# Two sixteen-head attentions of a four-layer kernel: which tick takes which PSUM bank, and when the reciprocals are transposed

## The chip, the cores and the metric

The kernel runs on one core of one Trainium2 chip. The metric is the device time of one launch in microseconds (us). TensorE, VectorE, ScalarE, GpSimd and the DMA queue of SyncE each run a program of their own and wait for each other through semaphores; in the rows of the profile they are PE (matmuls) and PEld (weight loads), DVE, ACT, POOL and SP.

## The reference, cut to what matters

Four layers of a network with adaptive layer norms. Each layer is an attention and then a feed-forward part, on 16 sequences of 256 tokens with 128 channels. The change concerns the attentions of layers 0 and 1, which have 16 heads of 64 channels each:

```python
h = _layernorm(x) * (1 + ca) + sa             # one (ca, sa) for each sequence
q, k, v = split(h @ wqkv.T)                    # 16 heads x 64, T = 256
# layer 0: q, k = rope(rmsnorm(q) * wq), rope(rmsnorm(k) * wk); causal mask
# layer 1: no norm of q and k; a relative-position bias is added to the scores
p = softmax(q @ k.T / 8 (+ bias))
x = x + ga * ((p @ v) @ wo.T)
```

## The kernel before, in words

`wide_attention(layer)` writes the program of one such attention; `causal` is true for layer 0. The 16 sequences are the outer loop, the 8 pairs of heads the inner one, and one pair of heads of one sequence is a **tick**: t = 0 to 127, and two more ticks to drain. u = t % 8 is the tick's place in its **octet**, k = t // 8 the octet, which is also the sequence whose scores are made. On every engine the body of the loop over t stands written out in program order, so the order of the work around the change is the order of the calls in that loop, and nothing else plans it.

In tick t TensorE does, in this order: `tensor_sums` (only at u = 1: it transposes the 128x32 tile RC of reciprocals of the softmax sums of the sequence before, one 128x128 operation into a bank of PSUM, line 570); `tensor_project` (q and k of a sequence that comes two octets later for layer 0, one octet later for layer 1: one matmul of 512 columns or two of 256); `tensor_turn` (layer 0 only: four 128x128 transposes of the rotated q or k, line 562); `tensor_extra` (see below); `scores` of pair t; `turn` of pair t - 1 (line 629: transposes of the exponentials, 12 in layer 0, 16 in layer 1); `value` of pair t - 2. The records of a 4-byte matmul come in twos, so that a 512-column matmul counts two.

`tensor_extra` holds what not every tick has: a quarter of the values v of the next sequence in the ticks u of `v_at` = (2, 3, 4, 7); the output projection of the sequence before, `c0` at u = 6 and `c1` at u = 7, eight matmuls each; and, in every second octet at u = 7, the turn of a normed chunk of x (two sequences, four 128x128 transposes, line 242), which is here called the norm's turn. `norm_at(a, u)` says when; a is the sequence that is being projected.

**The ring.** Banks 0 to 3 hold the scores, bank 4 the values' product. Everything else, so each project, turn, v, c0, c1, reciprocals' turn and norm's turn, goes into banks 5, 6 and 7 in rotation. `take_tick` hands them out, in its own order, when the program is written: the n-th taking gets bank 5 + n % 3, and a writer waits until the use of the same bank three takings before has been emptied. A tick of layer 0 takes two banks for project and turn and one for each extra, so u = 7 takes four (project, turn, v, c1) and in every second octet five; a tick of layer 1 takes one less.

VectorE's tick is `vector_spread` (u = 1: copies the transposed reciprocals out of PSUM, line 738, after which SyncE sends them to DRAM and back, spread over the partitions, lines 1037 and 1043), `vector_project` (layer 0: two multiplications of 128x512, line 713), `vector_extra` (the gated output at u = 6 and 7, line 168; the even quarters of v, line 772; for a chunk of the norm the statistics at u = 0, lines 176 and 179, and the normed x at u = 3 and 4, line 231), then the row maxima (lines 784, 785 and 787 in layer 0; 802 and 807 in layer 1), at u = 0 the reciprocals (line 748), the copy of half of the turned exponentials (line 869), and in layer 0 the sums of squares (line 729). ScalarE's tick is `scalar_turn`, `scalar_project` (layer 0: the squares; this frees the projection's bank), `scalar_extra` (the odd quarters of v; the modulation of the norm's turn), the other half of the turned exponentials, all on line 157, and then the four exponentials of the pair (line 932). GpSimd adds the rotated halves (lines 976, 977), scales k (line 997), raises the mean squares to the power -1/2 (line 985), scales the output with the reciprocals at u = 3 and 4 (line 1011, four of 128x512) and adds the residual (line 171).

Three waits matter for what follows:

```python
# scores(p): pair p - 2 must have left the banks      e.wait_ge(even_out, ...); e.wait_ge(odd_out, ...)
# turn(p):   the exponentials of pair p are made       e.wait_ge(pair_exped, p0 + p + 1)
# tensor_sums: the reciprocals are made                e.wait_ge(recip_made, b0 + c + 1)
```

Of the kernel before, what the change touches and what calls it, by code (L numbers as in the profile page):

```python
# [81 lines left out]
def program(nc, dr, out, stages=STAGES):  # L82
    ctx = ExitStack()
    with ctx:
# [323 lines left out]
        def wide_attention(layer, opening=None):  # L408
# [12 lines left out]
            causal = layer == 0  # L421
# [31 lines left out]
            ring = BK[5:8]  # L453
# [5 lines left out]
            ahead = 2 if causal else 1  # L459
            v_at = (2, 3, 4, 7)  # L460

# [8 lines left out]

            def norm_at(a, u):

                return u == 7 and a % 2 == 1 and a < 15

# [6 lines left out]
            def take_tick(t, a, b, u, ring=ring):  # L481

                for step, c in posts(t):
                    if step == "turn":
                        take(step, c, ring=ring)
                if 0 <= a < 16:
                    take("project", a, u, ring=ring)
                if causal and 0 <= b < 16:
                    take("turn", b, u, ring=ring)
                if 0 <= b < 16 and u in v_at:  # L490
                    take("v", b, v_at.index(u), ring=ring)
                for step, c in posts(t):
                    if step in ("c0", "c1"):
                        take(step, c, ring=ring)
                if norm_at(a, u):
                    take("ln", (a + 1) // 2, ring=ring)

# [74 lines left out]
            def tensor_extra(e, t, a, b, u):  # L572
                if 0 <= b < 16 and u in v_at:
                    tensor_v(e, b, v_at.index(u))
                for step, c in posts(t):
                    if step in ("c0", "c1"):
                        qt = int(step[1])
                        s = slots[step, c]
                        e.wait_ge(chunk_scaled, c0 + 4 * c + 4)
                        bk = fill(e, s)  # L580
                        for j in range(8):
                            x = mm(e, bk[:, 0:128], OT[(4 * c + j // 2) % 6][:, j % 2, 128 * qt:128 * qt + 128], WO[:, j, :],
                                   j == 0, j == 7)
                        x.then_inc(s.full, 1)
                if norm_at(a, u):
                    norm.turn(e, (a + 1) // 2)

# [75 lines left out]
            def tensor(e):  # L663
# [18 lines left out]
                for t in range(last):  # L682
                    a, b, u = t // 8 + ahead, t // 8 + 1, t % 8
                    tensor_sums(e, t)
                    tensor_project(e, a, u)
                    tensor_turn(e, b, u)
                    tensor_extra(e, t, a, b, u)
                    if t < 128:
# [61 lines left out]
            def vector_extra(e, t, a, b, u):  # L750
# [8 lines left out]
                if 0 <= b < 16 and u in v_at[0::2]:  # L759
                    vector_v(e, b, v_at.index(u))  # L760
                if norm_at(a, 7):
                    if u == 0:
                        norm.stats(e, (a + 1) // 2)
                    elif u in (3, 4):
                        norm.normed(e, (a + 1) // 2, 2 * u - 6, 2 * u - 4)

# [67 lines left out]
            def vector(e):  # L834
# [20 lines left out]
                for t in range(last):  # L855
                    a, b, u = t // 8 + ahead, t // 8 + 1, t % 8
                    vector_spread(e, t)
                    vector_project(e, a, u)
                    vector_extra(e, t, a, b, u)
# [47 lines left out]
            def scalar_extra(e, a, b, u):  # L907
                if 0 <= b < 16 and u in v_at[1::2]:
                    scalar_v(e, b, v_at.index(u))
                if norm_at(a, u):  # L910
                    c = (a + 1) // 2
                    if c >= 2:
# [74 lines left out]
            def gpsimd_tick(e, t, a, b, u):  # L987
# [10 lines left out]
                if causal and 0 <= a < 16:  # L998
                    gpsimd_add(e, a, u)
                    if u == 6:  # L1000
                        gpsimd_rstd(e, a, 0)
                if u == 1 and norm_at(a, 7):
                    norm.rstd(e, (a + 1) // 2)
                for step, c in posts(t):
# [2217 lines left out]
```

## Time and profile before

| | us |
|---|---|
| median of 3 runs | 3043.09 (3043.07 to 3043.55) |
| the profiled execution, its own time | 3035.05 |
| its span | 3033.3 |
| PE busy | 2791.1 (92%) |
| DVE, ACT, POOL busy | 2149.0 (71%), 1706.9 (56%), 1043.7 (34%) |
| attention of layer 0, ticks | about 63 to 680 |
| attention of layer 1, ticks | about 1067 to 1672 |

The span is what the profiler's rows cover; the execution's own time is 1.8 us longer. The ends of matmuls are modelled, so the starts of a kind of instruction that comes once in each tick tell the length of a tick better than the busy time does: in layer 0 the four transposes of line 562, which come right behind the projection, in layer 1 those of line 629.

### The profile page before, as it was taken

How to read it: one execution, taken by the hardware profiler on the slowest of the kernel's cores; microseconds unless marked ns; L12 is line 12 of the kernel's file. 1: busy time of each engine (PE TensorE's matmuls, PEld its weight loads, DVE VectorE, ACT ScalarE, POOL GpSimd, SP SyncE). 2: the span in 40 equal slices, each digit the busy share in tenths (PEclk: the TensorE clock that was granted, in tenths of full speed). 3: DMA queues.
4: the chain of work that ended last, by engine and by line, in shares of the span. 5: the costliest groups of instructions: out<-in, count | busy, mean ns of one | idle time of the engine just before them, and what ended most of it. 6: DMA issues, size and time to landing. Idle time of an engine off the chain costs nothing.

```text
span 3033.3 us, 68982 instructions
## 1 busy us (share of the span) xinstructions
PE 2791.1 (92%) x25484; PEld 1876.1 (62%) x25484; DVE 2149.0 (71%) x5792; ACT 1706.9 (56%) x4109; POOL 1043.7 (34%) x1420
## 2 busy tenths in 40 slices
PE   6999999989999999999998799999989988998897
PEld 2666666666666666666666455577756655556675
DVE  6888888855666566666666688665667786887674
ACT  3877777873333377777776466634335443333565
POOL 7787778731000001111112345222333321004341
PEclk9999999999999999999999899999989999999999
DMA  3110111122000011111112544100054432334660
GB/s 104 30 29 17 29 29 30 29 72 99 15 1 1 10 25 30 30 30 30 30 30 65 150 140 131 45 1 15 1 150 136 121 92 57 84 72 130 195 173 26
DMA packets 194061, 188.15 MB, mean 62 GB/s; under 512 B 14416, under 2 KB 170256, under 8 KB 192960
## 3 DMA queue, kind: packets, MB, share of 16 engines
q1 hardware_dynamic: 193728, 183.73, 23.2%
q8 instruction: 206, 3.38, 0.5%
q14 instruction: 127, 1.04, 0.1%
HBM read 130.36 MB, written 53.31 MB: 61 GB/s over the span
## 4 chain that ended last, share of the span: by engine, by line
PE 64%; DVE 18%; ACT 6%; issue 5%; SPq 3%; DMA 2%; POOL 2%; DVEq 0%; ACTq 0%; POOLq 0%
PE pb L160 57%; ACT big L932 4%; PE pb L629 3%; SPq L1834 2%; DVE big L2153 2%; ACT big L157 2%; DVE big L802 2%; DVE big L231 1%; DVE big L785 1%; DMA big<-parts 1%; PE pb L562 1%; DVE big L713 1%; PE pb L2124 1%; DVE big L784 1%; DVE big L176 1%
## 5 line engine op out<-in xcount | busy, mean ns | idle before, releaser
L160 PE MATMUL pb<-big 64*128 64x256 bf16 (+13 forms) x20300 | 2525.4, 331 | 157.9 <-DVE big L2153 59.1
L160 PEld LDWEIGHTS pb<-big 128*128 128x128 f32 (+5 forms) x20300 | 1576.6, 145 | 904.9 <-issue 537.5
L157 ACT ACTIVATE big<-pb 128x512 f32<-128x512 f32 (+7 forms) x1444 | 825.9, 619 | 573.9 <-PE pb L160 333.8
L157 ACT ACTIVATE big<-pb,big 128x512 f32<-128x512 f32 (+2 forms) x536 | 315.9, 616 | 607.4 <-PE pb L160 511.7
L2153 DVE TENSOR_REDUCE big<-pb 128x4 f32<-128x1024 f32 (+1 forms) x256 | 278.1, 1086 | 111.5 <-PE pb L160 108.2
L171 POOL TENSOR_TENSOR big<-big 128x128 f32<-128x128 f32 x192 | 85.0, 457 | 684.2 <-DVE big L168 684.2
L932 ACT ACTIVATE big<-big 128x256 f32<-128x256 f32 x512 | 253.9, 497 | 70.9 <-DVE big L807 69.1
L932 ACT ACTIVATE big<-pb,big 128x128 f32<-128x128 f32 (+1 forms) x512 | 255.6, 513 | 64.5 <-DVE big L787 64.2
L802 DVE CUSTOM_DVE_ANT_0 big<-pb,big 128x256 f32<-128x256 f32 x512 | 186.6, 421 | 80.2 <-PE pb L160 79.9
L1011 POOL TENSOR_TENSOR big<-big 128x512 f32<-128x512 f32 x128 | 159.8, 1276 | 243.2 <-DMA big<-recip 243.2
L1508 DVE SCALAR_TENSOR_TENSOR big<-pb,big 128x128 f32<-128x128 f32 x512 | 144.0, 344 | 139.3 <-PE pb L160 138.5
L1486 DVE SCALAR_TENSOR_TENSOR big<-pb,big 128x512 f32<-128x512 f32 x200 | 148.6, 749 | 90.0 <-PE pb L160 60.8
L184 POOL TENSOR_SCALAR big<-big 128x4 f32<-128x4 f32 (+1 forms) x104 | 27.3, 263 | 489.6 <-DVE big L179 489.6
L629 PEld LDWEIGHTS pb<-big 64*128 64x128 f32 x3584 | 146.1, 139 | 74.7 <-ACT big L932 57.7
L629 PE MATMUL pb<-big 64*128 64x64 f32 x3584 | 157.5, 225 | 26.7 <-ACT big L932 26.3
L985 POOL TENSOR_TENSOR big<-big 128x32 f32<-128x32 f32 x32 | 174.2, 5443 | 2.7
L713 DVE TENSOR_TENSOR big<-pb,big 128x512 f32<-128x512 f32 x256 | 163.9, 680 | 10.1 <-PE pb L160 7.8
L869 DVE COPY big<-pb 128x384 f32<-128x384 f32 (+1 forms) x256 | 156.9, 613 | 2.7 <-PE pb L629 2.7
L168 DVE TENSOR_TENSOR big<-pb,big 128x128 f32<-128x128 f32 x128 | 34.8, 288 | 129.8 <-PE pb L160 125.1
L976 POOL TENSOR_TENSOR big<-big 128x256 f32<-128x256 f32 x128 | 82.5, 644 | 87.8 <-DVE big L713 84.0
L562 PEld LDWEIGHTS pb<-big 128*128 128x128 f32 x512 | 63.2, 141 | 76.6 <-issue 68.7
L231 DVE TENSOR_SCALAR big<-big 128x128 f32<-128x128 f32 x256 | 97.8, 435 | 15.0 <-POOL big L186 11.7
(138 smaller groups left out, 2290.6 us busy)
## 6 DMA issues: line engine op xcount, KB each, us to landing
big<-parts SPq DMA_DIRECT2D x96, 512.0 KB, 4.1
parts<-big SPq DMA_DIRECT2D x384, 96.0 KB, 2.3
big<-recip SPq DMA_DIRECT2D x64, 512.0 KB, 6.5
big<-comb SPq DMA_DIRECT2D x32, 512.0 KB, 8.4
parts<-big SPq DMA_DIRECT2D x192, 64.0 KB, 2.1
big<-gates SPq DMA_DIRECT2D x8, 1024.0 KB, 6.2
big<-in_wf SPq DMA_DIRECT2D x1, 3072.0 KB, 14.9
big<-scratch SPq DMA_DIRECT2D x1, 3072.0 KB, 17.6
```

The lines of the kernel that those rows point to most:

```text
L157: return e.activation(o, i, f, bias=bias, scale=scale)
L160: return e.matmul(o, l, r_, start=start, stop=stop, skip_group_check=True)
L629: t = e.transpose(banks[2 * (p % 2) + half][:, 64 * at:64 * at + 64], PS[p % 2][rows, i, 128 * blk:128 * blk + 128], IDF[rows, rows])
L713: t = e.tensor_tensor(h3(D), h3(bk), TAB[:, 2 * qk + kk, tile, :].unsqueeze(1).to_broadcast([128, 8, 64]), ALU.mult)
L802: t = e.tensor_tensor_reduce(ps[:, i, x], banks[2 * (p % 2) + i][:, x], U[:, 2 * j + i, 128 - 128 * qt:384 - 128 * qt], 1.0, -3.0e38, ALU. ...
L869: e.tensor_copy(*turned_out(t - 1, 0)).then_inc(even_out, 1)
L932: t = e.activation(ps, banks[2 * s + i][:, at:at + w] if causal else ps, ACT.Exp, bias=NM[s][:, m:m + 1], scale=rstd_q(b)[:, qt, h:h + 1] ...
L985: e.tensor_tensor(half, half, HALF, ALU.pow).then_inc(rms_made, 1)
L1011: e.tensor_tensor(OT[k % 6], OT[k % 6], R[:, 2 * i:2 * i + 2, :], ALU.mult).then_inc(chunk_scaled, 1)
L1486: e.scalar_tensor_tensor(out=H[n % hn], in0=bk[:, :], scalar=B2[:, nf * u + f:nf * u + f + 1], in1=sg, op0=ALU.add, op1=ALU.mult).then_inc ...
L1508: x = e.scalar_tensor_tensor(out=ACC[s][:, i, :], in0=bk[:, 128 * i:128 * i + 128], scalar=CMB[s][:, E * i + u:E * i + u + 1], in1=ACC[s][ ...
L2153: e.tensor_reduce(m[:, :, 0:n, jj], two[:, :, 0:width].rearrange("p e (q x) -> p e q x", q=n), AXX, ALU.max, negate=True).then_inc(maxed, 1)
```

## The change

It does four things, in both attentions. (1) `v_at` becomes (2, 3, 4, 5): the last quarter of v moves from u = 7 to u = 5 on TensorE and on ScalarE. (2) The norm's turn, and its modulation on ScalarE, move from u = 7 of an octet with odd a to u = 0 of the same octet; the statistics and the normed x of that chunk move eight ticks ahead, into the octet before (a even), so that the first chunk that this concerns is normed in layer 0's first octet (k = 0) and, for layer 1, in the part of the kernel before it, whose last steps host the attention's start. Chunk 0, and chunk 1 of layer 0, stay at u = 7. `normed_in` and `turned_in` take the place of `norm_at`. (3) The reciprocals' turn comes behind project and turn on TensorE, in the ring's order, and on VectorE, where the copy now stands behind `vector_project`. (4) With that, no tick of layer 0 takes more than three banks of the ring.

```diff
--- before.py
+++ after.py
@@ -457,7 +457,7 @@
             last = 128 + 2
             guests_at = 120 if causal else 112
             ahead = 2 if causal else 1
-            v_at = (2, 3, 4, 7)
+            v_at = (2, 3, 4, 5)
 
             def take(*key, ring=ring):
                 slots[key] = ring[taken[0] % len(ring)].use()
@@ -468,9 +468,17 @@
                 return [(step, t // 8 - 1) for step, late in (("recip", 0), ("turn", 1), ("scale0", 3), ("scale1", 4), ("c0", 6), ("c1", 7))
                         if t >= 8 and t % 8 == late]
 
-            def norm_at(a, u):
-
-                return u == 7 and a % 2 == 1 and a < 15
+            def normed_in(a):
+
+                if a == -1 or causal and a == 1:
+                    return (a + 1) // 2
+                return a // 2 + 1 if 2 * (ahead - 1) <= a < 14 and a % 2 == 0 else None
+
+            def turned_in(a, u):
+
+                if a == -1 or causal and a == 1:
+                    return (a + 1) // 2 if u == 7 else None
+                return (a + 1) // 2 if a < 15 and a % 2 == 1 and u == 0 else None
 
             def begun(step, first=-1, stop=ahead):
 
@@ -480,20 +488,20 @@
 
             def take_tick(t, a, b, u, ring=ring):
 
-                for step, c in posts(t):
-                    if step == "turn":
-                        take(step, c, ring=ring)
                 if 0 <= a < 16:
                     take("project", a, u, ring=ring)
                 if causal and 0 <= b < 16:
                     take("turn", b, u, ring=ring)
+                for step, c in posts(t):
+                    if step == "turn":
+                        take(step, c, ring=ring)
                 if 0 <= b < 16 and u in v_at:
                     take("v", b, v_at.index(u), ring=ring)
                 for step, c in posts(t):
                     if step in ("c0", "c1"):
                         take(step, c, ring=ring)
-                if norm_at(a, u):
-                    take("ln", (a + 1) // 2, ring=ring)
+                if turned_in(a, u) is not None:
+                    take("ln", turned_in(a, u), ring=ring)
 
             norm = Norm(own_v, own_g, MODS[layer % 2], 0, slots, r0)
 
@@ -582,8 +590,8 @@
                             x = mm(e, bk[:, 0:128], OT[(4 * c + j // 2) % 6][:, j % 2, 128 * qt:128 * qt + 128], WO[:, j, :],
                                    j == 0, j == 7)
                         x.then_inc(s.full, 1)
-                if norm_at(a, u):
-                    norm.turn(e, (a + 1) // 2)
+                if turned_in(a, u) is not None:
+                    norm.turn(e, turned_in(a, u))
 
             def tensor_v(e, b, n):
                 tile, half = n // 2, n % 2
@@ -681,9 +689,9 @@
                         e.wait_ge(bank.free, n)
                 for t in range(last):
                     a, b, u = t // 8 + ahead, t // 8 + 1, t % 8
-                    tensor_sums(e, t)
                     tensor_project(e, a, u)
                     tensor_turn(e, b, u)
+                    tensor_sums(e, t)
                     tensor_extra(e, t, a, b, u)
                     if t < 128:
                         scores(e, t)
@@ -758,11 +766,12 @@
                         residual_vector(e, r0 + qt, qt, bk[:, 0:128], 0).then_inc(s.free, 1)
                 if 0 <= b < 16 and u in v_at[0::2]:
                     vector_v(e, b, v_at.index(u))
-                if norm_at(a, 7):
+                c = normed_in(a)
+                if c is not None:
                     if u == 0:
-                        norm.stats(e, (a + 1) // 2)
+                        norm.stats(e, c)
                     elif u in (3, 4):
-                        norm.normed(e, (a + 1) // 2, 2 * u - 6, 2 * u - 4)
+                        norm.normed(e, c, 2 * u - 6, 2 * u - 4)
 
             def vector_v(e, b, n):
                 tile, half = n // 2, n % 2
@@ -854,8 +863,8 @@
                         e.wait_ge(s.free, s.n)
                 for t in range(last):
                     a, b, u = t // 8 + ahead, t // 8 + 1, t % 8
+                    vector_project(e, a, u)
                     vector_spread(e, t)
-                    vector_project(e, a, u)
                     vector_extra(e, t, a, b, u)
                     if t < 128:
                         if causal:
@@ -907,8 +916,8 @@
             def scalar_extra(e, a, b, u):
                 if 0 <= b < 16 and u in v_at[1::2]:
                     scalar_v(e, b, v_at.index(u))
-                if norm_at(a, u):
-                    c = (a + 1) // 2
+                c = turned_in(a, u)
+                if c is not None:
                     if c >= 2:
                         s = slots["v", 2 * c - 3, 3]
                         e.wait_ge(s.full, s.n)
@@ -999,8 +1008,8 @@
                     gpsimd_add(e, a, u)
                     if u == 6:
                         gpsimd_rstd(e, a, 0)
-                if u == 1 and norm_at(a, 7):
-                    norm.rstd(e, (a + 1) // 2)
+                if u == 1 and normed_in(a) is not None:
+                    norm.rstd(e, normed_in(a))
                 for step, c in posts(t):
                     if step in ("scale0", "scale1"):
                         half = int(step[5])
```

TensorE at u = 7, u = 0 and u = 1 of layer 0's first octet with an output projection (k = 1). Rows 333 to 338 of the program before are the tick u = 7 up to its scores; line 160 with 128x512 is a projection or a quarter of v, with 128x128 x7 the output projection; `free5` is the wait until bank 5 has been emptied:

```order
L160 MATMUL pb<-big 128x512 [waits free5]
L562 MATMUL pb<-big 128x128 [waits free6,k_scaled]
L562 MATMUL pb<-big 128x128 x3
L160 MATMUL pb<-big 128x512 [waits free7]
L160 MATMUL pb<-big 128x128 [waits free5,chunk_scaled]
L160 MATMUL pb<-big 128x128 x7
```

The same tick now (lines 562, 570 and 629 have become 570, 578 and 637):

```order
L160 MATMUL pb<-big 128x512 [waits free6]
L570 MATMUL pb<-big 128x128 [waits free7,k_scaled]
L570 MATMUL pb<-big 128x128 x3
L160 MATMUL pb<-big 128x128 [waits free5,chunk_scaled]
L160 MATMUL pb<-big 128x128 x7
```

The quarter of v is gone. The output projection waited for the bank of this tick's own projection, and now waits for bank 5, which the tick before used last, for its own output projection.

The beginning of the tick u = 1, before:

```order
L570 MATMUL pb<-big 32x128 [waits free5,recip_made]
L160 MATMUL pb<-big 128x512 [waits free6]
L562 MATMUL pb<-big 128x128 [waits free7,q_rotated]
L562 MATMUL pb<-big 128x128 x3
L160 MATMUL pb<-big 128x2x128 [waits odd_out,even_out]
```

and now:

```order
L160 MATMUL pb<-big 128x512 [waits free6]
L570 MATMUL pb<-big 128x128 [waits free7,q_rotated]
L570 MATMUL pb<-big 128x128 x3
L578 MATMUL pb<-big 32x128 [waits free5,recip_made]
L160 MATMUL pb<-big 128x2x128 [waits odd_out,even_out]
```

The wait for the reciprocals stands behind the projection and its turn, directly ahead of the scores.

VectorE from u = 0 to u = 1 of an octet of layer 0 in which a chunk is normed, as it is now (721 was 713, 746 was 738, 756 was 748, 793 and 794 were 784 and 785):

```order
L721 TENSOR_TENSOR big<-pb,big 128x512
L176 BN_STATS big<-big 128x6 [waits ld_x4]
L176 BN_STATS big<-big 128x6 x3
L179 BN_AGGR big<-big 128x2 [waits wide_v0]
L179 BN_AGGR big<-big 128x2 x3
L793 TENSOR_REDUCE big<-pb 128x2 [waits rms_made,pair_exped,pair_scored]
L794 TENSOR_REDUCE big<-pb 128x2
L796 TENSOR_TENSOR big<-big 128x4 [waits wide_v0]
L756 RECIPROCAL big<-big 128x32 [waits full5,pair_exped]
```

The statistics stand where they stood, between the projection's multiplications and the row maxima, but in the other octet: the one that has no norm's turn.

## Rows read from the trace of the kernel before

**Rows 1.** The page, part 4: the chain that ended last, shares of the span by engine.
```profile
PE 64%; DVE 18%; ACT 6%; issue 5%; SPq 3%; DMA 2%; POOL 2%; DVEq 0%; ACTq 0%; POOLq 0%
```
**Rows 2.** Busy times in two stretches: layer 0, octets 1 to 12; layer 1, octets 1 to 13.
```profile
core 0: us, PE busy (x) PEld busy (x) DVE busy (x) ACT busy (x) POOL busy (x), PEclk, DMA share, GB/s
95.40:573.22 477.82, 446.50 (x4165) 294.54 (x4164) 400.12 (x817) 374.95 (x1141) 380.53 (x375) 1.00 0.14 28
1105.97:1596.25 490.28, 481.13 (x4303) 331.96 (x4301) 329.21 (x1303) 346.89 (x1130) 84.14 (x90) 1.00 0.15 30
```
**Rows 3.** PE's waits in layer 0, 68 to 660 us: in total, times, longest.
```profile
PE pb L160 <- ACT big L157: 12.8, 13, 1.0
PE pb L629 <- ACT big L932: 12.7, 22, 1.6
PE pb L570 <- DVE big L748: 10.7, 13, 1.4
```
**Rows 4.** The same in layer 1, 1060 to 1660 us.
```profile
PE pb L629 <- ACT big L932: 8.3, 27, 1.8
PE pb L160 <- DVE big L869: 5.1, 6, 1.9
```
**Rows 5.** Timeline of PE, octets 4 and 5 of layer 0: start us, us, instruction, [idle before].
```profile
215.59 0.60 PE L562 MATMUL pb<-big 128*128 128x128 f32 x4
...
219.75 0.60 PE L562 MATMUL pb<-big 128*128 128x128 f32 x4
...
223.40 0.60 PE L562 MATMUL pb<-big 128*128 128x128 f32 x4
...
236.94 0.60 PE L562 MATMUL pb<-big 128*128 128x128 f32 x4
...
241.62 0.60 PE L562 MATMUL pb<-big 128*128 128x128 f32 x4
...
247.06 0.60 PE L562 MATMUL pb<-big 128*128 128x128 f32 x4
...
254.57 0.60 PE L562 MATMUL pb<-big 128*128 128x128 f32 x4
...
258.78 0.29 PE L570 MATMUL pb<-big 128*32 128x128 f32 x1 [1.38 <-DVE big L748]
...
259.76 0.60 PE L562 MATMUL pb<-big 128*128 128x128 f32 x4
...
287.30 0.60 PE L562 MATMUL pb<-big 128*128 128x128 f32 x4
...
289.75 2.02 PE L160 MATMUL pb<-big 128*128 128x128 f32 x16 [0.98 <-ACT big L157]
...
295.25 0.60 PE L562 MATMUL pb<-big 128*128 128x128 f32 x4
```
**Rows 6.** Timeline of DVE in octet 5, which norms a chunk.
```profile
254.87 1.29 DVE L713 TENSOR_TENSOR big<-pb,big 128x512 f32<-128x512 f32 x2
...
257.27 0.39 DVE L784 TENSOR_REDUCE big<-pb 128x2 f32<-128x256 f32 x1
...
276.17 0.41 DVE L784 TENSOR_REDUCE big<-pb 128x2 f32<-128x256 f32 x1
```
**Rows 7.** Chain of waits, octet 5: the end of tick u = 4's exponentials and its turn.
```profile
277.81 1.73 ACT big L932 x7
...
279.58 0.59 PE pb L629 x12
```
**Rows 8.** Timeline of DVE in layer 1's octet 4, the normed x of two ticks.
```profile
1226.26 2.62 DVE L231 TENSOR_SCALAR big<-big 128x128 f32<-128x128 f32 x2
...
1232.39 0.59 DVE L231 TENSOR_SCALAR big<-big 128x128 f32<-128x128 f32 x2
```
**Rows 9.** Timeline of POOL at the same place.
```profile
1226.29 4.97 POOL L1011 TENSOR_TENSOR big<-big 128x512 f32<-128x512 f32 x4 [10.80 <-DMA big<-recip]
```

## The prediction, blind

> **What bounds the kernel now.** I began with the chain that ended last: 64% of it is TensorE, 18% VectorE [rows 1]. Only the two attentions change, so next came the busy times of their steady parts. Layer 0's octets 1 to 12 take 477.82 us, 39.82 each, with PE busy 446.5 of them and DVE 400.1; layer 1's octets 1 to 13 take 490.28 us, 37.71 each, with PE busy 481.1 [rows 2]. Layer 0 thus has 31 us in which TensorE stands still, layer 1 only 9. PE's waits name layer 0's: 13 waits for a bank that ScalarE empties (12.8 us), 22 for the exponentials (12.7), 13 for the reciprocals (10.7) [rows 3]; layer 1 has 8.3 us for exponentials and 5.1 for VectorE's copy [rows 4]. The last view is the timeline of PE, where the starts of line 562 give each tick's length [rows 5]:
>
> - u = 1, with nothing extra, takes 223.40 - 219.75 = 3.65. That is a **bare tick**: I take it as TensorE's own work, since no wait is shown in it.
> - u = 2, 3, 4, each with a quarter of v: 236.94 - 223.40 = 13.54, so 4.51 each, and a quarter of v costs 0.86.
> - u = 5 has nothing extra but takes 4.68: 1.03 of waiting.
> - u = 6 takes 5.44, so the output projection costs 1.79.
> - u = 7 takes 7.51 where 3.65 + 0.86 + 1.79 = 6.30 is work: 1.21 of waiting. In octet 5 it takes 7.95, and the row at 289.75 shows the bank's wait ahead of the output projection. The norm's turn is the 0.44 between.
> - u = 0 up to the next line 562, with the reciprocals' turn in it, takes 4.16 in octet 4 and 5.19 in octet 5, so 0.51 and 1.54 above a bare tick. In octet 5 the row at 258.78 shows 1.38 of it as a wait for the reciprocals; the remaining 0.16 is the operation.
>
> TensorE's work in an octet is therefore 8 x 3.65 + 4 x 0.86 + 2 x 1.79 + 0.16 = 36.4 us, 36.8 with a norm's turn; octet 4 takes 38.98, octet 5 takes 40.68.
>
> But TensorE is not alone at the bound. Octet 5 norms a chunk, and VectorE, between the multiplications that begin u = 0 at 254.87 and the row maxima of u = 4 at 276.17, works practically without a pause [rows 6]; the exponentials of u = 4 follow, and TensorE's turn of them starts only when they end, at 279.58 [rows 7]. The statistics alone push the row maxima of u = 0 to 257.27, 1.29 us of multiplications and 1.1 of statistics behind 254.87.
>
> **The change part by part.**
>
> *The last quarter of v, from u = 7 to u = 5.* No work is added or removed: 0.86 leaves u = 7 and arrives at u = 5, where 1.03 is waiting anyway. In an octet that norms nothing this takes 0.86 off u = 7 and leaves u = 5 at 4.51, plus the 0.17 of its waiting that v does not fill. I take the 0.17 as gone; at worst it stays, 0.17 x 13 = 2 us. On ScalarE the copy moves too, out of the tick in which the bank's wait ended on it.
>
> *The ring.* At u = 7 the output projection asks for the bank of the tick before, where VectorE has to finish one product. That product has a whole tick of 5.4 us of time, so the 1.21 of waiting at u = 7 goes. New waits could come from the other end: with three takings per tick, each projection takes the bank of the projection before it. ScalarE must have squared it; TensorE comes to it after the turn and the value product of the same tick, as it already does at u = 3 and 4, which take their 4.51 without a wait. I cost it at nothing, with that cover.
>
> *The reciprocals' turn behind projection and line 562.* These are 0.86 + 0.44 = 1.3 us of TensorE work, taking a projection as long as a quarter of v (both are one 512-column matmul). The wait was 1.38 in octet 5 [rows 5] and 10.7 / 13 = 0.82 in the mean [rows 3], so nearly all goes. VectorE's copy also stands later and can't stop the multiplications any more. Queued behind the wait now are the scores of u = 1. The round trip through DRAM starts 1.3 us later; the rival below costs that.
>
> *The norm's turn at u = 0.* 0.44 on TensorE, moved. On ScalarE the modulation now stands ahead of the exponentials of u = 0 instead of u = 7. Octet: 36.8.
>
> *The norm's statistics and products, an octet ahead.* Their work now falls in the octets without a norm's turn, and VectorE's own sequence from u = 0 to u = 4 is the same as in octet 5. So 254.57 to 287.30, 32.73 us from the start of u = 0 to that of u = 7 [rows 5], stays; the new quarter of v at u = 5 fits into TensorE's waiting. Only u = 7 shrinks, from 7.95 to 5.44. That makes **38.2** us; I take 38.0, since the copy of the reciprocals stops VectorE no more.
>
> Sum for layer 0: octets 1 to 12 are six with a norm's turn (36.8), five that norm (38.0) and one with neither (36.4): 447.2 instead of 477.8, **-30.6**. Octet 0 takes over one chunk's norm, 38.0 - 36.4 = 1.6, of which its own waiting at u = 5 covers a little: **+1.4**. Octet 13 loses its waits, 1.21 + 1.03 + 0.35: **-2.5**. The last two octets, without projections, stay. Layer 0: **-31.7**. From below: were VectorE the bound in every octet as in those that norm, octets 1 to 12 would take 12 x 38.0 = 456.0, and layer 0 would gain 22. From above: no wait at all, each octet at TensorE's work, would gain 40.
>
> Layer 1. VectorE is busy 329 of 490 us, so it has room. The same quarter of v fills what is waiting at u = 5, and the reciprocals' wait is small already. All its shown waits are 13.4 us [rows 4]; that is the most it can give, and 0 the least unless something new comes (below). I take **-5**, nearer to the lower end, because the waits for VectorE's copy come from another cause, the port (below). Chunk 1's norm now runs in the last steps of the expert part before it, where I cost it at nothing: VectorE's 3 us there stand beside TensorE's matmuls.
>
> Total: -36.7. Against the profiled execution's own 3035.05 this is 2998.4; the median of the runs is 8.0 us above that execution, and I take the gain from it: 3043.09 - 36.7 = **3006.4**.
>
> **A rule against it.** In layer 1 the two normed tiles of one tick took 2.62 us where they took 0.59 a tick later [rows 8]. They began at 1226.26, GpSimd's scaling at 1226.29 [rows 9]. The products of a norm now stand in the other octets and the scaling comes later in the tick, so they may miss each other or meet oftener. I price no change, and 2.03 us for a meeting. The Trainium skill, page SBUF — State Buffer, section "Who interferes with whom", says that VectorE and GpSimd share one port pair by an exclusive lock, so that the second of the two blocks for the whole of the other's instruction. By that rule the trace agrees with the 2.62, and every overlap of line 231 with line 1011 would cost up to one instruction of GpSimd; its sum here is that of the first rival, below.
>
> **Rivals.** (0.2% of the time, 6 us, is about what a measurement of this kernel can tell from no change.)
>
> 1. *The norm meets the scaling.* In each of six octets of both layers 2.03 us are added to VectorE's sequence at u = 3 or 4, where it is the bound or near it: 12 x 2.03 = 24, so 3031. For: rows 8. Against: octet 5 had both in the same ticks and VectorE's sequence already holds what that cost; in layer 1 some octets pay it now.
> 2. *The waits move.* TensorE comes earlier to the turn of the exponentials, and waits there instead. Only u = 7's 1.21 is kept, 13 times: -16, so 3027. For: 22 such waits exist [rows 3], and VectorE has work 84% of the time. Against: in octet 4 three ticks in a row take their bare 4.51.
> 3. *Slower.* The reciprocals leave 1.3 us later for DRAM, and the scaling, hence the output projection at u = 6, waits for them. In octet 5 the turn of the reciprocals is at 258.78, and u = 6 and 7 are ticks with an output projection, the second beginning at 287.30. In layer 1 four scalings end 4.97 after 1226.29 [rows 9]. It decides only if the trip takes some 5 us more than now. To end slower it has to cost the 36.7 and another 6 over about 28 octets, so 1.5 us each: 3050 or more.
> 4. *The bank was not the cause*: ScalarE itself is late at u = 7, and the scores or the next projection wait for it as the output projection did. All stays within 6 us of 3043.
> 5. *More than forecast*: the octets that norm reach 36.4 as well, and layer 1 gives 10: -50, so 2993.
>
> **How the numbers follow.** Forecast 0.61, spread 2996 to 3021 by the bounds of its terms (layer 0 from -22 to -40, layer 1 from 0 to -7); rival 1 0.12, rival 2 0.13, rival 3 0.04, rival 4 0.05, rival 5 0.05. Faster by more than 0.2% is the forecast with rivals 1, 2 and 5: 0.91; within it rival 4, 0.05; slower rival 3, 0.04. The range of 2990 to 3029 leaves out rivals 3 and 4, about half of rival 1, and the far end of rival 5: about 0.17.
>
> **What would show it.** In the profile of the changed kernel, layer 0: the bank's wait at u = 7 and the reciprocals' wait gone from PE's waits; u = 5, 6, 7 at about 4.5, 5.4, 5.4 us; octets alternating between about 36.8 and 38.0, with what is left in waits for the exponentials in those that norm; layer 1's octets near 37.3. It is wrong if layer 0's octets stay above 39, if the waits for exponentials grow by what the others lose, if line 231 takes over 2 us in many octets, or if an output projection waits for the scaled chunks.

## The result, and the profile after

| | before | changed |
|---|---|---|
| median, us | 3043.08 (4 runs, 3035.17 to 3043.55) | 3007.74 (4 runs, 3002.56 to 3011.66) |
| span of the profiled execution | 3033.3 | 3009.9 |
| last turn of exponentials of layer 1 (PE), us from the start | 1671.5 | 1641.6 |
| from there to VectorE's first operation on the last residual products (line 2928, now 2937) | 1357.6 | 1364.1 |

The ratio of the times is 0.9889, 95% interval 0.9867 to 0.9911. The medians are 35.3 us apart; 36.7 were forecast. The two profiled executions are only 23.4 us apart, and the table says why: the attentions end 29.9 us earlier, and 6.5 us are lost behind them, in stages that the change doesn't touch (the last section).

The page of the changed kernel, part 4, with more of the chain on TensorE and less on VectorE than [rows 1]:

```profile
PE 67%; DVE 15%; ACT 6%; issue 5%; SPq 3%; DMA 2%; POOL 2%; DVEq 0%; ACTq 0%; POOLq 0%
```

The same two stretches as [rows 2], layer 0's octets 1 to 12 and layer 1's 1 to 13 (columns: PE, PEld, DVE, ACT, POOL busy, granted clock, DMA share, GB/s):

```profile
97.80:548.84 451.04, 444.79 (x4165) 294.15 (x4164) 393.59 (x805) 372.11 (x1141) 379.60 (x373) 1.00 0.15 30
1080.72:1567.06 486.34, 479.46 (x4303) 333.13 (x4303) 328.21 (x1295) 345.67 (x1130) 82.80 (x88) 1.00 0.15 30
```

PE's busy time has hardly moved (446.5 to 444.8 us); 25 of the 26.8 us that layer 0's twelve octets gave are time in which PE stood still. What is left of PE's waits in layer 0, 68 to 633 us, for [rows 3]:

```profile
PE pb L637 <- ACT big L941: 10.2, 19, 2.0
```

The 13 waits for a bank (12.8 us) and the 13 for the reciprocals (10.7) are gone, and beside the row above the list has only 1.4 us for VectorE's copy (line 878); the waits for the exponentials went only from 12.7 to 10.2. This list holds gaps of more than 0.15 us; shorter ones show in the lengths of the ticks. The timeline of PE shows where they are now. First an octet with a norm's turn, u = 0 to the start of u = 2; then one that norms a chunk:

```profile
248.19 0.60 PE L570 MATMUL pb<-big 128*128 128x128 f32 x4
...
252.28 0.60 PE L570 MATMUL pb<-big 128*128 128x128 f32 x4
252.72 0.27 PE L578 MATMUL pb<-big 128*32 128x128 f32 x1
...
254.59 0.59 PE L637 MATMUL pb<-big 64*128 64x64 f32 x12 [0.62 <-ACT big L941]
...
256.88 0.60 PE L570 MATMUL pb<-big 128*128 128x128 f32 x4
...
285.80 0.60 PE L570 MATMUL pb<-big 128*128 128x128 f32 x4
...
287.47 0.59 PE L637 MATMUL pb<-big 64*128 64x64 f32 x12
...
289.82 0.60 PE L570 MATMUL pb<-big 128*128 128x128 f32 x4
...
294.32 0.60 PE L570 MATMUL pb<-big 128*128 128x128 f32 x4
```

In the first octet u = 0 takes 4.09 us and u = 1 4.60, in the second 4.02 and 4.50. TensorE's work in them would be 4.09 and 3.81 in the first, 3.65 and 3.81 in the second. The reciprocals' turn (line 578) waits for nothing; the turn of u = 0's exponentials behind it does. The rest of the octets is nearly as forecast: u = 5 at 4.5 to 4.7 (once 5.04), u = 6 and 7 at 5.44 and 5.43, in place of 4.68, 5.44 and 7.51 [rows 5].

In the second octet u = 0 is 0.37 above its work too. Its turn, at 287.47, comes 1.67 us behind line 570; in the kernel before it came 1.42 behind line 562 in each of octets 2 to 13. What it had to wait for is the end of u = 7's exponentials on ScalarE, at 287.41:

```profile
287.21 0.20 ACT L941 ACTIVATION_READ_ACCUMULATOR big<-pb,big 128x1 f32 x1
```

With u = 7 at 5.43 in place of 7.51, TensorE arrives before them, in each of octets 2, 4, 6, 8, 10, 12 and 13. Where the norm's turn stands in u = 0 its 0.44 fills the time (4.08 to 4.10 us, all of it work). Why u = 1 waits differs between the two octets. On ScalarE in the first, the modulation of the norm's turn stands ahead of the exponentials:

```profile
251.12 1.06 ACT L157 ACTIVATE big<-pb,big 128x256 f32<-128x256 f32 x2
252.02 0.54 ACT L157 ACTIVATE big<-pb 128x384 f32<-128x384 f32 x1
252.40 0.52 ACT L941 ACTIVATE big<-pb,big 128x128 f32<-128x128 f32 x1
```

VectorE had the maxima's product ready at 251.48, ScalarE begins at 252.40. On VectorE in the second it is the statistics, as in [rows 6]:

```profile
287.48 0.86 DVE L176 BATCH_NORM_STATS2 big<-big 128x6 f32<-128x128 f32 x4
...
288.67 0.39 DVE L793 TENSOR_REDUCE big<-pb 128x2 f32<-128x256 f32 x1
```

Layer 1 gave 3.9 us in its thirteen octets (490.28 to 486.34) and lost 1.0 in the octet ahead of them. Its waits, for [rows 4], 1034 to 1633 us, with 3.0 us for VectorE's copy in place of 5.1:

```profile
PE pb L637 <- ACT big L941: 9.9, 27, 1.9
```

### The profile page after: what moved, and what is told of

The parts are those of the page before. It is cut to its first block, busy times and chain, and to the rows that moved or that the text cites. A ratio compares the mean times of both kernels' runs of the same rounds, so it can differ in the third digit from the quotient of the medians.

```text
span 3009.9 us, 68983 instructions
## 1 busy us (share of the span) xinstructions
PE 2799.5 (93%) x25484; PEld 1882.5 (63%) x25484; DVE 2145.4 (71%) x5792; ACT 1703.0 (57%) x4109; POOL 1041.7 (35%) x1420
## 4 chain that ended last, share of the span: by engine, by line
PE 67%; DVE 15%; ACT 6%; issue 5%; SPq 3%; DMA 2%; POOL 2%; DVEq 0%; ACTq 0%; POOLq 0%
PE pb L160 60%; ACT big L941 4%; PE pb L637 3%; SPq L1843 3%; ACT big L157 2%; DVE big L2162 2%; DVE big L811 2%; DMA big<-parts 1%; PE pb L570 1%; DVE big L231 1%; PE pb L2133 1%; DVE big L176 1%; DVE big L1495 1%; DVE big L2652 1%; DVE big L721 1%
## 5 line engine op out<-in xcount | busy, mean ns | idle before, releaser
L160 PE MATMUL pb<-big 64*128 64x256 bf16 (+12 forms) x20300 | 2535.0, 332 | 141.2 <-DVE big L2162 58.3
L637 PE MATMUL pb<-big 64*128 64x64 f32 x3584 | 157.9, 225 | 26.3 <-ACT big L941 25.3
L721 DVE TENSOR_TENSOR big<-pb,big 128x512 f32<-128x512 f32 x256 | 163.9, 681 | 12.8 <-PE pb L160 11.0
L941 ACT ACTIVATION_READ_ACCUMULATOR big<-pb,big 128x1 f32 x512 | 110.5, 216 | 0.0
L231 DVE TENSOR_SCALAR big<-big 128x128 f32<-128x128 f32 x256 | 98.0, 437 | 14.9 <-POOL big L186 11.6
```

The source lines that it names most:

```text
L160: return e.matmul(o, l, r_, start=start, stop=stop, skip_group_check=True)
L637: t = e.transpose(banks[2 * (p % 2) + half][:, 64 * at:64 * at + 64], PS[p % 2][rows, i, 128 * blk:128 * blk + 128], IDF[rows, rows])
L721: t = e.tensor_tensor(h3(D), h3(bk), TAB[:, 2 * qk + kk, tile, :].unsqueeze(1).to_broadcast([128, 8, 64]), ALU.mult)
L941: t = e.activation(ps, banks[2 * s + i][:, at:at + w] if causal else ps, ACT.Exp, bias=NM[s][:, m:m + 1], scale=rstd_q(b)[:, qt, h:h + 1] ...
```

## The experiments

Ten kernels have one execution each, and two have five. A whole execution wanders by several us with the granted clock of stages that no experiment touches, so the single ones are read by octets 1 to 12 of layer 0, octets 1 to 13 of layer 1 and the time of layer 1's last turn. How well these repeat is told by two kernels of which two executions were profiled: the octets by 0.4 to 0.7 us, the last turn only by 2.9 and 5.9 us, because a part without change lies ahead of it too.

| kernel | layer 0, 1 to 12 | layer 1, 1 to 13 | last turn | us |
|---|---|---|---|---|
| before | 477.82 | 490.28 | 1671.5 | 3035.1 |
| changed | 451.04 | 486.34 | 1641.6 | 3011.7 |
| v at 5 only | 455.67 | 488.08 | 1647.6 | 3007.1 |
| v at 6 only | 484.43 | 491.12 | 1679.3 | 3053.7 |
| reciprocals' turn only | 473.04 | 492.37 | 1673.0 | 3038.5 |
| changed, reciprocals back | 455.98 | 486.21 | 1644.3 | 3011.6 |
| changed, norm back | 449.47 | 485.53 | 1635.9 | 3008.6 |
| changed, modulation on VectorE | 448.05 | 484.47 | 1637.6 | 3011.7 |
| changed, statistics late | 450.27 | 486.96 | 1641.5 | 3007.5 |
| changed, both | 448.25 | 487.26 | 1637.9 | 3008.5 |
| changed, norm at u = 5 to 7 | 447.99 | 484.80 | 1635.9 | 3006.3 |
| that, modulation on VectorE | 445.65 | 484.19 | 1631.4 | 2993.2 |
| changed, second execution | 450.46 | 485.65 | 1638.7 | 3010.9 |
| last kernel, second execution | 446.37 | 484.60 | 1637.3 | 3009.1 |

**v at u = 5, nothing else.**

```diff
-            v_at = (2, 3, 4, 7)
+            v_at = (2, 3, 4, 5)
```

> The kernel before with one part of the change: the last quarter of v at u = 5 instead of u = 7; norm and reciprocals' turn stay. Theory (each wait is its own: the bank's wait at u = 7 comes from the fourth taking of the ring in one tick, and u = 5 had room): in layer 0, u = 7 falls from 7.51 to 5.44 us (with a norm's turn from 7.95 to about 5.9, up to 6.3), u = 5 falls from 4.68 to 4.5 to 4.6, the ticks u = 0 keep their wait for the reciprocals (4.16 and 5.19); octets 1 to 12 take 452 to 455 us instead of 477.8. Layer 1 gains 3 to 5 us. Rival (the waits only move: TensorE waits for exponentials elsewhere): octets 1 to 12 at 462 or more.

Measured: octet 4 takes 4.16, 3.65, 4.51, 4.51, 4.52, 4.69, 5.44, 5.44 us, octet 5 begins with 5.37 and ends with 6.12. PE's waits in layer 0:

```profile
PE pb L570 <- DVE big L748: 9.7, 12, 1.5
PE pb L629 <- ACT big L932: 4.3, 8, 1.6
```

The bank's wait is gone and the reciprocals' wait stays, as the theory said; the twelve octets take 455.7 us, just outside its 452 to 455, with u = 0 behind a short u = 7 at 5.37 where 5.19 was expected. Layer 1's thirteen octets gave 2.2 us, less than the 3 to 5. This one number moved makes 22 of the changed kernel's 27 us in layer 0's octets.

**v at u = 6.**

```diff
-            v_at = (2, 3, 4, 7)
+            v_at = (2, 3, 4, 6)
```

> The kernel before, with the last quarter of v at u = 6 instead of u = 7. Then u = 6 takes four banks and u = 7 three (four with a norm's turn), and u = 5 stays with nothing extra. If the ring's fourth taking is the cause: the wait of about 1 us moves to u = 6 (about 7.5 us), u = 7 is 5.44 (5.9 with a norm's turn), u = 5 stays at 4.68, and octets 1 to 12 stay at 477 plus or minus 3 us. Rival (the copy of v on ScalarE at u = 7, or something else about u = 7, is the cause, not the number of banks): u = 6 takes 6.3 us, no bank's wait is shown, and octets 1 to 12 take about 463.

Measured: u = 6 takes 7.93 us, u = 7 5.43 (6.12 with a norm's turn), u = 5 4.68. The wait went along with the fourth taking; first TensorE's row, then ScalarE's:

```profile
247.73 2.46 PE L160 MATMUL pb<-big 128*128 128x128 f32 x22 [1.40 <-ACT big L157]
```

```profile
246.00 2.07 ACT L157 ACTIVATE big<-pb 128x512 f32<-128x512 f32 x4
```

It is 1.40 us instead of 0.98, and the octets take 484.4 us, more than the 477 plus or minus 3 expected: at u = 6 ScalarE has one operation of 0.6 us more ahead of the squares, and nothing is won at u = 5. The copy of the quarter of v moved along with the taking, so the length alone does not part the two; the rows do. By their semaphores the four operations of ScalarE are the copy of the values' product, the copy of the turn, the squares that free the projection's bank, and the copy of the quarter of v. The squares end at 247.58, TensorE goes on at 247.73, and the copy of v ends only at 248.07; in [rows 5] the squares end at 289.60, TensorE goes on at 289.75, the copy ends at 290.09. So it is the ring that makes the wait. The quarter of v must go to a tick with a bank and time to spare, not only away from u = 7.

The number of takings does not give the size of the wait. In octets with a norm's turn u = 7 still takes four banks here, and in the kernel with v at 5: it takes 6.12, where the work is 5.44 + 0.44, so 0.24 of waiting. There the fourth taking comes behind 1.79 us of output projection, at u = 6 and in the kernel before behind 0.86 of v.

**The reciprocals' turn alone.** `tensor_sums` behind `tensor_turn`, `vector_spread` behind `vector_project`, and the ring's order with them, in the kernel before.

> The kernel before with only the reciprocals' turn moved behind the tick's projection (TensorE, VectorE and ring). Theory: the wait for the reciprocals, 10.7 us in all, goes, but behind it stands the turn of u = 0's exponentials, which are hardly earlier; in octets that norm, half of the gain is taken back there. Octets 1 to 12 at 470 to 473 us instead of 477.8. Rival A (nothing behind it): 467. Rival B (the wait moves as a whole): 476 or more.

Measured: 473.0, a gain of 4.8 us in layer 0's octets. The 10.7 us of waits vanish from the list, and those for the exponentials grow from 12.7 to 14.5:

```profile
PE pb L629 <- ACT big L932: 14.5, 28, 1.0
```

In the octets that norm, u = 0 and u = 1 go from 5.19 and 3.65 to 3.73 and 4.62: of 1.46 us 0.97 come back a tick later, two thirds where half was expected. In the others, 4.16 and 3.65 become 3.72 and 3.76, and 0.12 to 0.25 more is lost at u = 4. Layer 1's thirteen octets are 2.1 us longer than before, and its last turn comes 1.5 later: what layer 0 won does not show at the end of the attentions.

**The changed kernel with the reciprocals' turn back.**

> The changed kernel with the reciprocals' turn back at the head of u = 1. The changed kernel's octets 1 to 12 of layer 0 take 451.0 us. If the parts are independent this one loses what the move alone gains in the kernel before, 5 to 8 us: 456 to 459. Rival (behind the move stands the wait for u = 0's exponentials, so that with the other parts in place it is worth little): 451 to 453.5.

Measured: 455.98, of which one octet with 39.97 instead of 38.4 makes 1.6. Against the changed kernel's two executions, 451.0 and 450.5, that is 4.9 and 5.5 us, or 3.3 and 3.9 without this octet: the move is worth 3 to 5.5 us with the other parts, at the lower edge of the first expectation or between the two. Added to v alone (22.2), 4.8 gives 27.0, and the whole change gave 26.8; the next experiment shows that the two parts together gave more than that sum.

**The changed kernel with the norm back** in the octets with odd a, and its turn at u = 7:

```diff
+            def normed_in(a):
+                return (a + 1) // 2 if a % 2 == 1 and a < 15 else None
+            def turned_in(a, u):
+                return (a + 1) // 2 if a % 2 == 1 and a < 15 and u == 7 else None
```

> The changed kernel, with the norm's statistics, products and turn back in the octets with odd a and the turn at u = 7. Theory: the move of the norm shifts work between octets and brings little: the octets without any of it take 36.7 to 37.1 us, those with all of it 38.3 to 38.9, octets 1 to 12 of layer 0 450 to 454 us in place of 451.0. Rival (the norm's turn as the fourth bank of u = 7 still costs a wait of 1 us, and VectorE's sequence as before another): 456 or more.

Measured: 449.5, octets of 36.7 to 36.8 and 38.1 (the first 38.5). The norm's turn as a fourth bank of u = 7 costs 6.12 - 5.44 - 0.44 = 0.24, no more. Against the changed kernel's two executions the octets of layer 0 are 1.0 and 1.6 us shorter, those of layer 1 0.1 and 0.8: **the move of the norm brought nothing**. In layer 0 it rather costs about 1 us, and octet 0, which has one chunk's norm more by it, takes 34.7 in both executions instead of 32.9. The moves of v and of the reciprocals' turn, which this kernel has alone, give 28.4 us in octets 1 to 12. The reason for the cost is in the ticks u = 1: here they take 4.49 in the octets with odd a and 3.76 in the others, in the changed kernel 4.59 and 4.50, so that nearly all octets wait and not every second. The last turn, 5.7 and 2.8 us earlier, repeats too badly to say that it costs.

**Modulation on VectorE.** In ticks u = 0 the two operations are made by VectorE, ahead of its row maxima:

```diff
+                if c is not None and not u:
+                    norm.modulated_vector(e, c, lambda n: HT[c % 2][:, 256 * n:256 * n + 256])
...
+                    t = e.tensor_scalar(dst(i), s.t[:, 256 * i:256 * i + 256], self.mod[:, self.which + 1, b:b + 1],
+                                        self.mod[:, self.which, b:b + 1], ALU.mult, ALU.add)
```

> The changed kernel, but the modulation of the norm's turn at u = 0 is made by VectorE (two operations of 128x256) instead of ScalarE. Theory: in the changed kernel's octets with a norm's turn, u = 1 takes 4.59 us instead of 3.8, because the modulation, 1.06 us, stands ahead of u = 0's exponentials on ScalarE. Without it u = 1 falls to 3.8 to 3.9 in those six octets and octets 1 to 12 of layer 0 fall from 451.0 to 446 to 448; layer 1's six such octets, with 4.35 at that place, fall to 3.8 too, 3 us in all. Whole kernel 6 to 8 us faster than the changed one. Rival (VectorE's row maxima of u = 0 become late instead): no gain, u = 1 at 4.4 to 4.6.

Measured: 448.05, at the edge of the 446 to 448. In octet 5, u = 1 falls from 4.60 to 4.15, not to the 3.8 expected; the octet from 37.60 to 37.20. The modulation's place on ScalarE was the cause of half of that wait, 0.44 of 0.78 us; the other half is not explained by this run. Layer 1's octets are 1.2 to 1.9 us shorter, but not at this place: the six ticks of 4.35 fell to 4.05, not to 3.8, and six of 3.8 rose to 4.05. The whole run shows nothing of it (3011.7, where 6 to 8 us less were expected): from layer 1's last turn on it took 1367.9 us, where the changed kernel's took 1364.1.

**Statistics behind the sums of squares.**

```diff
-                    if u == 0:
+                    if u == 0 and t < 0:
                         norm.stats(e, c)
...
                     vector_squares(e, a, u)
+                    if u == 0 and normed_in(a) is not None:
+                        norm.stats(e, normed_in(a))
```

> The changed kernel, with the statistics of a chunk behind VectorE's sums of squares of u = 0 instead of ahead of its row maxima. In the octets that norm, u = 1 (4.50 us) waits for exponentials that the statistics delay. Theory (VectorE's whole sequence from u = 0 to u = 4 is the bound in these octets): u = 1 falls to about 3.9 but u = 2 to 5 grow by as much; octets 1 to 12 within 1 us of 451.0. Rival (only u = 0's order counts): 4 us less, 447.

Measured: 450.27, within 1 us (0.8 and 0.2 less than the changed kernel's two), and octet 4 takes 4.01, 4.15, 4.64, 4.50, 4.54, 4.71 up to u = 5 instead of 4.01, 4.49, 4.51, 4.52, 4.50, 4.58: what u = 1 gives, the next ticks take. That fits VectorE's sequence as the bound, and not the order at u = 0.

**Both.**

> The changed kernel with both edits: modulation at u = 0 on VectorE and the statistics behind the sums of squares. If both kinds of octet have their own cause of the wait at u = 1, octets 1 to 12 of layer 0 take 442 to 445 us; if VectorE's sequence is the bound in the octets that norm, 446 to 448, as with the modulation alone.

Measured: 448.25, as with the modulation alone: the second expectation, missed by a quarter of a us.

**The norm at u = 5 to 7.** If VectorE's sequence over u = 0 to 4 is the bound, its work has to leave those ticks. Statistics at u = 5, normed tiles at u = 6 and 7:

```diff
+            def norm_tick(a, u):
+                if a == -1 or causal and a == 1:
+                    return {0: "stats", 1: "rstd", 3: 0, 4: 2}.get(u)
+                return {5: "stats", 6: 0, 7: 2}.get(u)
```

> The changed kernel with the norm's work on VectorE at other ticks of the same octet: statistics at u = 5 (from u = 0), the normed tiles at u = 6 and 7 (from u = 3 and 4), GpSimd's part at u = 5; the norm's turn stays at u = 0 of the next octet, on ScalarE. Theory (VectorE's sequence from u = 0 to u = 4 is the bound in octets that norm, and u = 6 and 7 have room): in layer 0 u = 1 of these octets falls from 4.50 to 3.8, the octets that norm take 36.7 to 37.0 us, those with the norm's turn stay at 37.6; octets 1 to 12 from 451.0 to 445 to 447. In layer 1 no normed tile meets the scaling by the reciprocals, u = 4 falls from 4.5 to 5.1 us to about 4.5: octets 1 to 13 from 486.3 to 482 to 484. The last turn of layer 1, at 1641.6 us in the changed kernel, comes 8 to 12 us earlier. Rival (the waits move to other ticks): within 3 us.

Measured: octet 4 takes 4.02, 3.76, 4.51, 4.50, 4.51, 4.51, 5.44, 5.43, 36.7 in all: u = 1 is where TensorE's own work puts it. The octets that norm take 36.7 to 37.0 us, as expected; u = 0 stays at 4.02, behind u = 7's exponentials. Those with the norm's turn take 37.7 to 38.1 from octet 3 on, where 37.6 was expected. The twelve octets take 448.0 (445 to 447 expected), layer 1's thirteen 484.8 (482 to 484), and the last turn comes 2.8 to 5.7 us earlier, not 8 to 12. Layer 1 disappointed: u = 4 still takes up to 5.12 us, though no normed tile is near the scaling any more.

> The same with the modulation of the norm's turn at u = 0 on VectorE. Theory: besides, u = 1 of the octets with a norm's turn falls from 4.59 to about 4.15; the last turn of layer 1 comes 11 to 16 us earlier than the changed kernel's 1641.6. Rival: no more than with the other ticks alone.

With the modulation on VectorE as well: 445.65 (446.4 in the second execution), octet 5 37.09 with u = 1 at 3.99; in octets 3, 7, 9 and 11 u = 1 takes the 4.15 expected. The last turn at 1631.4 and 1637.3 us is 1.4 to 10.2 us earlier than the changed kernel's, so the 11 to 16 expected did not come; the octets, which repeat, gave 4.1 to 5.4 in layer 0 and 1.1 to 2.2 in layer 1. PE stands still for 1.4 of layer 0's 445.65 us:

```profile
97.32:542.97 445.65, 444.25 (x4165) 294.35 (x4164) 401.09 (x817) 368.01 (x1130) 378.33 (x373) 1.00 0.15 30
```

**Five executions each** of the last kernel and the changed one, on the same chip:

> The kernel with the norm's work at u = 5 to 7 and the modulation on VectorE, timed. Theory: its two attentions are some 12 us shorter than the changed kernel's, so that it runs 40 to 48 us faster than the kernel before, 2993 to 3003 us. Rival (the single look was a matter of the granted clock, which moves the untouched stages by several us): no more than 36 us faster, as the changed kernel.

> The changed kernel itself, timed beside the other on the same chip: 3003 to 3012 us, 31 to 40 us faster than the kernel before.

Measured: the last kernel 2998.15 us (2990.37 to 3009.09), ratio to before 0.9858 (0.9835 to 0.9880); the changed kernel 3008.70 (3003.71 to 3012.03), ratio 0.9888 (0.9870 to 0.9906); before 3040.26 in nine runs. The last kernel is ahead of both in the median, by 42.1 and 10.6 us. Its interval still touches the changed kernel's, and of the 10.6 us the octets show about 6, so that a lead over the changed kernel is shown in the octets, while its size in the whole is not settled.

## Why the prediction was right, and where it was not

*The reading of what bounds the kernel* held. Of the three waits of [rows 3] that it was built on, the ring's came from the fourth taking of a tick, which v at u = 6 and its rows show; u = 5 had the time for a quarter of v, which v at u = 5 shows.

*Size of layer 0*: -31.7 forecast, -26.6 measured (its last turn from 678.0 to 651.4). By octets 1 to 12: -26.8 instead of -30.6. The step that failed is "The norm's turn at u = 0. ... Octet: 36.8", which noted that the modulation now stands ahead of u = 0's exponentials and cost it at nothing: these octets took 37.6, 0.8 us more, which makes 4.8 us in six of them. The modulation on VectorE gave half of it back. The text took a bare tick's 3.65 as reachable whenever TensorE has nothing else, but at u = 1 the exponentials of u = 0 come only if VectorE and ScalarE were on time. The five octets that norm were 1.5 us better than forecast, and octet 12, with neither, 0.6 worse: 4.8 - 1.5 + 0.6 is the 3.9 that the twelve octets missed.

*The octets that norm*: 38.0 forecast, 37.5 to 38.0 measured, 37.7 in the mean. That VectorE's sequence from u = 0 to 4 bounds them is shown by the statistics moved late (no gain) and the norm's work moved out of these ticks (36.7 to 37.0 us).

*The reciprocals' turn*: the text said that nearly all of the wait goes. It did, but 0.97 of 1.46 us came back a tick later in the octets that norm; alone it brought 4.8 us of 10.7.

*Two small waits taken as gone stayed.* Without the norm's turn u = 0 was put at a bare 3.65 us and takes 4.02, as TensorE now comes to u = 7's exponentials before they are done. At u = 5 the 0.17 that v does not fill stayed in five of the twelve octets. Octet 12 has both: 36.99 where 36.4 was forecast.

*Octet 0 and octet 13*: +1.4 forecast, +2.0 measured in octet 0 (its end comes 2.4 later, as it also begins 0.4 later); -2.5 forecast, -2.0 measured.

*Layer 1*: -5 forecast, -3.6 measured (1670.7 to 1640.8 us by its last turn's start, less the 26.3 at its first). Its octets with a norm's turn have the same new wait at u = 1: 4.35 us where the others have 3.8. The text laid the waits for VectorE's copy to the port; they went from 5.1 to 3.0 us, and no run tests what makes them.

*The sum*: the last turn of layer 1 comes 29.9 us earlier in one execution and 32.8 in the other, and the medians differ by 35. The few us between are not shown to be the change's: the untouched stages wander by more. By its parts the forecast was 36.7 and the attentions gave 29.9 to 32.8, so that a median within 1.4 us of it is in part luck.

*Rivals.* The waits did not move as a whole (rival 2), though a part did, to u = 0 and u = 1. The bank was the cause (against rival 4): v at u = 5 alone brings u = 7 to 5.44. The norm meets the scaling (rival 1) was half right: in layer 1 every pair of normed tiles at u = 4 now overlaps the scaling by the reciprocals. Timeline of VectorE and of GpSimd in the changed kernel:

```profile
1312.32 0.60 DVE L231 TENSOR_SCALAR big<-big 128x128 f32<-128x128 f32 x2
...
1317.61 1.59 DVE L231 TENSOR_SCALAR big<-big 128x128 f32<-128x128 f32 x2
```

```profile
1313.86 5.00 POOL L1020 TENSOR_TENSOR big<-big 128x512 f32<-128x512 f32 x4 [12.21 <-DMA big<-recip]
```

Six such pairs take 1.14 to 1.75 us instead of 0.59, 5.3 us more in all; before, the meetings were fewer and longer, up to 2.62 [rows 8], and came to 5.7 in the six octets. The sum was as priced, none. Slower (rival 3): in the changed kernel no wait of TensorE for the scaled chunks is shown. More than forecast (rival 5) did not come: the octets that norm reached 36.7 only with the norm's work in other ticks.

## What to carry to other kernels

When several buffers rotate through a ring in program order, count the takings of each step of the loop. A step that takes one more than the ring has asks for the buffer of its own first use; what that costs depends on the work that lies between and on how late the engine that empties it comes: here 1.21 and 1.64 us behind a quarter of v, 0.24 behind an output projection. One item moved to a step with a free buffer and idle time can be nearly the whole gain. Behind each wait that is removed, look for the next one on the same engine and price it; here it was the exponentials, and work moved in front of them on ScalarE or VectorE gave back what it was moved to save. Read what each part of a change gave by itself: of this one, a single number gave four fifths of the gain in layer 0's octets, and the move of the norm gave nothing.

## What was not expected of the hardware

The stages that no kernel here touches are not equally long in two executions. From the same place to the same place, the third expert part, before and in the changed kernel (the two columns at 0.94 and 0.92 are the granted clock):

```profile
2524.20:2735.30 211.10, 189.87 (x953) 121.01 (x952) 168.51 (x462) 72.03 (x111) 23.27 (x42) 0.94 0.31 65
```

```profile
2496.10:2713.00 216.90, 195.81 (x954) 123.97 (x953) 167.81 (x458) 72.04 (x111) 21.87 (x39) 0.92 0.30 64
```

The second is 5.8 us longer, and PE is busy 5.9 us longer with the same matmuls. In the kernel with v at 5 the same stretch took 211.1 at 0.94. Over all profiled executions, the time from layer 1's last turn to VectorE's first operation on the last residual products lay between 1353.3 and 1368.2 us. These 14.9 us are more than any edit of the changed kernel did. Why the clock is granted otherwise is open; no run here was made for it.

In layer 1, the tiny product of the row maxima (128x4, 0.17 us) took 0.5 to 1.3 us in nearly every octet, once and only while GpSimd's scaling runs, in the kernel before, the changed one and the last one. In the kernel with the norm at u = 5 to 7 the length of u = 4 follows it: 5.12 us with a product of 1.23, 4.91 with 1.03, 4.54 with 0.66, and 4.50 in octet 2, where it took less than 0.4. So it seems to be what keeps u = 4 above 4.5 us there; it was not moved away, and that is not shown by an edit.
